# Another order of turns for five instruction streams in a 32-unit fused kernel

## The reference

```python
x = x + L0_attn(layernorm(x))   # 16 heads; q and k become spike counts (0 to 4) in 4 steps
x = x + L0_ffn(layernorm(x))    # gated, inputs, weights and hidden values rounded to FP4 in blocks of 16
x = x + L1_attn(layernorm(x))   # four Mamba layers, below
x = x + L1_ffn(layernorm(x))    # ternary weights, hidden size 512, silu and gelu
x = x + L2_attn(layernorm(x))   # causal linear attention, 16 heads
x = x + L2_ffn(layernorm(x))    # 8 experts, hidden size 512, top 1
x = x + L3_attn(layernorm(x))   # long convolution as a scan, gelu, projection, norm
x = x + L3_ffn(layernorm(x))    # dense part plus product-key experts
```

```python
u  = silu(conv(x @ Wi.T));  dt, B, C = split(u @ Wx.T);  dt = softplus(dt @ Wdt.T + bdt)
h  = exp(dt * A) * h + dt * B * u        # step by step over 256 tokens, 256 channels x 16 states
y  = (h * C).sum(states) + u * Dp;       out = (y * silu(z)) @ Wo.T + x
```

## Time and profile before

| what | us |
|---|---|
| median of 3 runs | 1852.78 |
| lowest, highest run | 1848.98, 1853.91 |
| span of the profiled execution | 1849.7 |
| PE busy | 1481.9 (80%) |
| DVE busy | 1499.8 (81%) |
| ACT busy | 1345.1 (73%) |
| POOL busy | 1196.0 (65%) |
| mean granted clock of TensorE | 0.879 of 2.4 GHz |

### The profile page before, as it was taken

The page is one execution under the profiler, slowest core; times in us unless marked ns, Lnnn a source line. Parts: engine busy times, 40 slices in busy tenths (PEclk is TensorE's granted clock), DMA queues, the critical chain, the costliest instruction groups (busy, mean ns, idle before and its releaser), DMA issues.

```text
span 1849.7 us, 27473 instructions
## 1 busy us (share of the span) xinstructions
PE 1481.9 (80%) x9417; PEld 1054.5 (57%) x9417; DVE 1499.8 (81%) x2326; ACT 1345.1 (73%) x2733; POOL 1196.0 (65%) x999
## 2 busy tenths in 40 slices
PE   5767666667898998577778999778899987889975
PEld 2433333335676666454456787656667765667854
DVE  6589999999999899978898888888889999731254
ACT  4466756666988788767687978788888787654564
POOL 3247668667676688866665656788878778730046
PEclk6667877778999999777798999999999998889997
DMA  5022403423444434220244444341445432212300
GB/s 194 1 69 70 121 18 95 113 70 103 115 117 119 126 104 110 72 69 24 64 119 123 117 127 134 92 112 49 127 136 141 132 104 70 66 33 85 115 18 6
DMA packets 84585, 170.10 MB, mean 92 GB/s; under 512 B 9440, under 2 KB 14944, under 8 KB 84064
## 3 DMA queue, kind: packets, MB, share of 16 engines
q1 hardware_dynamic: 84448, 168.37, 33.4%
HBM read 99.12 MB, written 2.10 MB: 55 GB/s over the span
## 4 chain that ended last, share of the span: by engine, by line
PE 42%; DVE 22%; ACT 19%; POOL 7%; issue 6%; DMA 3%; SPq 1%; DVEq 0%; POOLq 0%; ACTq 0%
DVE m L1051 8%; ACT m L1026 6%; DVE dtuB L1043 5%; PE ps L1080 4%; PE ps L1182 4%; PE ps L1467 3%; PE ps L1476 3%; PE ps L1314 3%; PE ps L965 3%; DMA m<-m 3%; PE ps L1764 3%; ACT L347 2%; PE ps L698 2%; PE ps L1325 1%; PE ps L711 1%
## 5 line engine op out<-in xcount | busy, mean ns | idle before, releaser
L1061 POOL TENSOR_TENSOR m<-m 128x1024 f32<-128x1024 f32 x256 | 777.2, 3040 | 162.8 <-DVE m L1051 161.1
L1051 DVE TENSOR_TENSOR_SCAN m<-m,dtuB 128x1024 f32<-128x1024 f32 x256 | 584.5, 2283 | 22.7 <-ACT m L1026 9.3
L1026 ACT ACTIVATE m<-m,Aneg 128x255 f32<-128x255 f32 x1024 | 431.7, 499 | 26.0 <-DMA m<-m 18.2
L1043 DVE TENSOR_TENSOR dtuB<-m 128x1024 f32<-128x1024 f32 x256 | 348.9, 1363 | 9.7 <-DMA m<-m 3.2
L1467 PE MATMUL ps<-o 128*128 128x256 f32 x512 | 150.8, 406 | 17.9 <-DVE X L1411 7.1
L1080 PE MATMUL ps<-m,w_const 128*32 128x256 f32 x2048 | 154.6, 432 | 12.1 <-POOL m L1061 12.1
L1434 ACT ACTIVATE o<-ps,w_mo 128x256 f32<-128x256 f32 x256 | 114.8, 472 | 54.9 <-PE ps L1467 54.0
L364 POOL TENSOR_TENSOR o<-o,mhalf 128x2 f32<-128x2 f32 x64 | 19.6, 306 | 200.0 <-DVE o L358 199.9
L965 PE MATMUL ps<-m,wc 128*128 128x256 f32 x512 | 134.3, 421 | 7.4 <-ACT m L385 7.3
L1476 PE MATMUL ps<-o 128*128 128x128 f32 x1024 | 130.6, 281 | 4.9 <-ACT o L1434 4.1
L1476 PEld LDWEIGHTS ps<-o 128*128 128x128 f32 x1024 | 124.5, 195 | 14.8 <-ACT o L1434 9.5
(11 more groups left out here) (251 smaller groups left out, 2920.1 us busy)
## 6 DMA issues: line engine op xcount, KB each, us to landing
m<-m SPq DMA_DIRECT2D x256, 256.0 KB, 4.8
m<-spread SPq DMA_DIRECT2D x64, 512.0 KB, 4.8
o<-in_mox SPq DMA_DIRECT2D x128, 256.0 KB, 2.9
o<-in_l1x SPq DMA_DIRECT2D x88, 256.0 KB, 2.9
w_mb<-in_mb SPq DMA_DIRECT2D x1, 2288.0 KB, 11.7
m<-in_cwr SPq DMA_DIRECT2D x1, 2048.0 KB, 15.8
w_l3f<-in_l3f SPq DMA_DIRECT2D x1, 1536.0 KB, 17.5
X<-in_x SPq DMA_DIRECT2D x4, 256.0 KB, 6.4
```

What stands on the lines that cost most here:

```text
L1026: op = e.activation(dA[at % NA][:, j, 1:CH], R[q][:, h * CH + 1:h * CH + CH], ACT.Exp, scale=Aneg[:, l, 4 * g + j:4 * g + j + 1])
L1043: e.tensor_tensor(dtuB[:, :, :], bc(R[q][:, (2 + h) * CH:(3 + h) * CH].unsqueeze(1), 4, CH), Br[k % 2], ALU.mult).then_inc(S.dve, n.tick(f ...
L1051: e.tensor_tensor_scan(flat(G[at % NG]), flat(dA[at % NA]), flat(dtuB[:, :, :]), 0.0, ALU.mult, ALU.add).then_inc(S.dve, n.tick(f"s{g}"))
L1061: e.tensor_tensor(G[at % NG], G[at % NG], Cr[k % 2], ALU.mult).then_inc(S.pool, n.tick(f"c{g}"))
```

## The change

Only the five strings of `ORDER` differ. The number of turns of each line on each engine is the same, and so are instructions, waits, tiles and DMAs, except table loads: ACT has 188 of them in its stream before (with one for each change of set) and 187 now. The first lines of two of the strings:

```diff
     "pe":
-        "a9ua2ua3ba2ba7bab2ab8ab2ab2ab5a3bab2a2f2b3faf2bab2abasa4b2a3fa2f2af2sa2bab2abab2asb2fab4sfabfsaf2bfsb2fsab2af2af3"
+        "a15uaubaba6b2abab8ab2a2b7a3bab2a2f2b2abf3ab3aba8fbaba2f3sfa2sab4a2b2sab2fab3asb2fafbsf3sb3fsa2f4bafb2sa2ba2babas"
...
     "dve":
-        "aua7u2bu3b7a11ba2fb2fb3a7b5fb2fs3fsbs2bs2bs4b2sb2fs8fs2af2s8a2sfa2fasf2s4as5a2sa2fs2abas2bs3a2bafasabababs2f2s6b"
+        "a2ua4uauab6ub2aua5ua5ba2fb2fb3a7b5fb2fs3fs9b7sfs8fs2fafs9a2fa2fasf2s8as2a4fs2a2bs2b2s3b3a3f3a4s9bs2b4fs7fs3f2sas8"
```

More of the change, by code:

```diff
@@ L214 @@
+        "s3fs4b5f3sbs5b2s2b2s4f2sfs6f2sfs4afsf2s7a5f3a2s8a4f3bs2b2s6b4f3s6b3sbsa3bafafa2sfs7a6fb2a2fabs8b2fb10f2s3bsfs4f2"
+        "a4s5a3fa3s2a2sf2sfs6b4sf3b2s2b2s3bsbs2a3b2a2faf2s4as2as2f3a2s8a3bafb2f2asbsbs4basb2sb2fb2fsbsfsbsbsbs3fs5fs2fsa12"
+        "b12a12ba2b2abab13a",
     "pe":
-        "a9ua2ua3ba2ba7bab2ab8ab2ab2ab5a3bab2a2f2b3faf2bab2abasa4b2a3fa2f2af2sa2bab2abab2asb2fab4sfabfsaf2bfsb2fsab2af2af3"
-        "b2sa3bab2a2safbabasa5fafbfa2fsfa6sa2fasaf2b2sfafafb2sb2fa2fsfbf2bfb2sb8sb2afsb4fsf3bfbsfsa2bf3asf2b2asfa2sbababa2"
@@ new lines @@
+        "afasb3fabafa3fabfba2fa2sab2a2ba2b2a2ba3b3a2sb2abababa2fababa2fba2fbabafafabfbs2ba2b2a5b5sbabfb4ab2fb2fb2fab3afabf"
+        "b2a2b2abasb3sab2ab8sa2fba3f2bf2afasa2bababa2sb2a2b2a2sa2fa3b2a2f2b4afasfa2bsfa4b2a3bab2asabafba2bfafbabfafafs2b2"
+        "a2b2sbabafba2babasafafsfafafbabasa2fb2a2b3fa2fbfasfb2a2fsbab3ab4sabfa2babf2ab2sa2fafa2b2fb2sb3aba2b3ab2sab2fb6afb"
+        "fbsb2fa2fsfab6ab5sb2afb4fsa3bafafafafsba4baba2b3sabafbsa5b2a5b4aba3sa3b3ababsa3fa3bab2a2ba3ba3b2abababab2ababa5b"
+        "a2b3aba2b2a2ba2b3a2b3ab3a3b2a2baba4baba3bab5aba2b2a3b6ab3a2bab4ab11ab8a2ba3ba2b3ab2ab2a5b7a2baba2b3",
@@ new lines @@
+    "dve":
+        "a2ua4uauab6ub2aua5ua5ba2fb2fb3a7b5fb2fs3fs9b7sfs8fs2fafs9a2fa2fasf2s8as2a4fs2a2bs2b2s3b3a3f3a4s9bs2b4fs7fs3f2sas8"
+        "a2fb2faf2a2sb7s10afs10fs2f2s9ba3f2af2s3fs13bafbafb3sf2safasbasab3sbs6fb2s7a2bfsf2s2a3b2sbas5fs10fs2f2as3babas3ab2"
+        "s2afsbabsfs2f2as8as4fsabsfs2af2b2s2abs4as3asabs2fba2s2bas2a2fbf2s8bs5bfa6fa2sf2as2bs3as2ba2s3b2sa6b2a2sfbas2b2sas"
+        "a2s3a2fs2f2sba6bfab2s2b4s2b2sb2fs4b8abs3fba2f2b2a2fab2sas4b7s8fa4fs2f2asas6as2as2bas2ab2fsb3fs3f2s2bs7b4a2fs2b2s4"
+        "a3fabf2b2s5bs4fs7af2asafs2babs2as4asb3fbsas4as5fas3f2asbs2ab3s2fabs2a2s2bfsaf2abasa2bs5bs4faba7bas3abs2ababfsf2ab"
+        "fsa5ba2sbasb2asasas3fa2s2a2s2as2ab6sb2f3bs3bfba2sbs4b4a2sab4abfs4b3sb2s3f3s2bs2bs2abs2a2s2fbs4as2fs2f2as8b2as3fba"
+        "bf3b2s5as8fs4as2fbf2s2babs2bs4bs2fas2bs4bfsaf2bs5bs6afabsba2s2fsabf2sa2bsbs6a3b2a6bsbabfasas3a5saba2fb2as2abfa2b2"
+        "s2a2b2s2baba2b2as4bs2b8sasab3sa3fbafb5a4b2abab3a2bab2ab2abab2a2babababa2b4aba2b2a6b3a2b3ab3a5b3a4b7ab2a2b3ab",
@@ new lines @@
+    "act":
+        "a11bua3u3baba5bab3ab5ab2a2b5aba2bafabf2ab2fbf2afbab2asasafa2sasfab2sfabas2f2af2a2bsb2sabsbsa2b2sbs2b2fafbs2f4ab2"
+        "s2afsbfs2af3asb2sfbsa3ba3sbs2bsa4fa2fasasbf2bf2asbsa3s2asa2s2a2f2s3fab2f3ab3fsfs2ba2f3sbsfbs3b4sbsb2s2b2sb4fbs2fs"
+        "af4s2afs2af2s2af2s2fbfba2sbsafa2bfabfs3a2fb2fa2bfsfs2a2sbababs2a3fafaba2bfabfsfas2fas2ababsasab2asas2asb2f2b2asfa"
+        "bafb3fsafa3bab3sba2sba2s2bafbabfs2ba2f2sbfsfa4b2asa2bas2a4fbfbsa4s2fba2fa2fsfb4a2b2s2b2asb2ab2sabasafb2abfs3fab2f"
+        "sfb2fbabasb2safbasb3fs2af2bab3asa2babf2bs2a2bas2ab2a2s2b2a2sab2faf2ba2safbabfsafasfab3a2ba2ba3ba2s2b2ab2abfbafbfb"
+        "as2fbafsfsfbsbsb8sb2asa2bsb2fsfsasabafabfs2fa2bfaba2sab2s3afafs2f2ba2fsfb3a2sa2b2s3a2ba2b2f2bafafsfas2afbabsasasa"
+        "bab2sas2babfbfasfabafab2fa2sfba2b2a2bsab2a2sabsab2sasba2bs2ba4bsfba2fsa2fbfabfba2fabsa4b3sbs2bababsbab2fb2fasbfa"
+        "b2fbasafab2fb2a3b4s2a2b4sb4a3babsfas2f2asbf2abfafa3sbabs2ba4b2a2bs2ba2sa3b2afa2bfbfbs2bafabfa2bfa2s2fa3b2sabababa"
+        "bs2basabsbaf2bs2afbfabfsfsab2asb2s2ab2sa2sb2sa2f2s2f2bafa2bfab2sa2b3asbfbfas3f2ba2fsbasafb2sb2sb2sasa3bf2s2babfa2"
+        "fasfbsfb2ab2saba2bsb3sb2sbsb3f2bs2fab2abfsfa2fbsb3abasb4as2b2ab2sf2a2sab2as2fafa2fsfba2ba2ba2b2a2bs3ba2b2a4s2a2b2"
+        "a2b2a2ba2bsba3bsa3b2sb2ababa7bab2a2b2a2ba2bab2ab3a2b2a2ba3b5ab2a3b2a2b3a2b3a2ba2ba4b2a4b5a4b7a2b2abab2ab3ab5ab4a"
+        "b4a3b2ababa2b3ababab2a3babab5a2b2a2babab3",
@@ L254 @@
+        "fbs5afas2a2sfs7fa4fa3sasasas2bsa2ba2fba4ba2s3asaf2sb4ab4s2b2fs3b9abf2b2s3bs5f2sas6bfs2fs4afsbs2asfs3fs5afsbs3bfs3"
+        "fs4bs2fs2afa2sas5fa7sa2sabfbsfsa4ba6bsfas5b3sbfb5fbsas3b4ab2sb3fbs2bsfs4asfs3fs4bs3f2bs6fs3fsbs4fs3fs6fasa2sfasb"
+        "s3ba5ba4bafs3a10b3sab6sbs4b9abs2ba2b3a4b4a10b10a8b4ab2ab4",
 }
```

43 lines of the change are left out of this document (6 added, 37 removed).

## The result

The changed kernel is slower: 1869.24 us at the median of its four runs (1866.63 to 1873.23) against 1853.1 us for the kernel before, run beside it (1848.98 to 1853.91). The ratio is 1.0096 with a 95% interval of 1.0077 to 1.0115: 14 to 21 us more, where I had forecast 8 us less. 1869.24 lies outside my range as well. The profiled execution took 1866.63 us, its span is 1864.8.

A forecast was written before the change was run, and what follows sets the result against it. DVE, busy 89% of the scan stage, was taken to set the pace; its terms of -10.7 us times 0.89 gave -9.5, with +0.5 and +1.0 -8.0: 1844.8 us from 1852.78, eight-in-ten range 1824 to 1861.

The forecast's parts named there:

- (a): First scan unit on DVE: turns of line b leave the gaps between groups, two held L1043 go; -4.3 us.
- (b): Other scan places with turns between L1051 and L1043: fewer holds of L1043 by new counts; -3.3 us, ends 0 and -10.1.
- (c): L838's waits on DVE at 898.95 and 1381.81 us are filled by other turns; -3.1 us, bounds -3.1 and +3.1.
- (d): Head on DVE: 25 setup instructions lose their covering wait and run ahead of L748; +0.5 us, ends 0 and +2.5.
- (e): POOL in the scans: L1061 takes 1.03 us longer at 14 more places; +1.0 us, ends 0 and +14.4.
- POOL takes over: Rival 2: in stretches of eight groups POOL has no time left, so the front comes late; +6.8 us, 1859.6, chance 0.09.
- the sum of +6.8 us: Scans, holds only moved between DVE and POOL: -7.6 us on DVE plus 14.4 us on POOL.
- (f): Table loads, one fewer of 188, nothing; tail, PE's work is the same and turns swap: 0, ends -3 and +3 us.
- The factor 0.89: DVE's busy share in the scan stage, taken as the part of its -10.7 us that counts: -9.5 us.
- the fifth: Whole order: turns are put ahead of others that are ready sooner, without the gains; +6.6 us, 1859.4, chance 0.05.
- rival 3: PE's granted clock falls to 0.69 in a scan stretch; +11 us, 1855 with the gain or 1864 without, chance 0.05.

The follow-up runs named there:

- e8_b_turns: Kernel before with one DVE move: seven turns of sequence 3's L0Attn stand together behind the first scan unit's sixth group; 0.9970, -5.6 us.
- e14_l838: Kernel before with seven DVE turns at 898.95 us in the new order, L409 and L411 ahead of L838 among them; 1.0014, +2.6 us.
- e10_act_1350: Kernel before with 23 ACT turns from 1348 us reordered, the first norm of unit 27's front five turns later; 1.0027, +5.0 us.
- e3_late: Kernel before with the new order of all engines from 1301 to 1630 us only (units 25 to 31); 1.0022, +4.1 us.
- e11_1682: Kernel before with the new order of all engines from 1682 to 1725 us only, in the tail; 1.0023, +4.3 us.
- e9_middle: Kernel before with the new order of all engines from 616 to 1301 us only (units 12 to 24); 1.0041, +7.6 us.

## Why the prediction was wrong

The mechanism I knew best was right, and it was a small part of the change. By my own steps:

- (a), -4.3: right in kind, sign and size. Both holds are gone; e8_b_turns gives -5.6 us, and unit 1's first L1043 starts at 148.27 there; I had said 147 to 148. In the changed kernel it starts at 153.84, 2.2 us later than before, because the first scan starts 7.7 us late: that hid the gain.
- (b), -3.3: wrong. L1043's excess over 1.232 us fell from 33.5 to 256 x (1.346 - 1.232) = 29.2 us, and these 4.3 us are no more than (a) alone. I had carried one mean per kind of place over to new places. In the changed kernel the places with one turn between have 0.48 instead of 0.60, those with two 0.20 instead of 0.10, and the 196 with none 0.10 instead of 0.09, 18 of them over 1.5 us instead of 13. Whether L1043 is held depends on where POOL is, not on the count of turns: of those over 1.5 us, 29 of 30 before and 28 of 28 now started while a POOL instruction had over 0.3 us still to run, and at the others that was so at 10 of 226 and 18 of 228.
- (c), -3.1 with bounds of ±3.1: the value wrong, and the bound far too tight. The wait at 898.95 fell from 3.82 to 2.00 us as I had said, and brought nothing (e14_l838). The place at 1381.81 became one of the worst: the front of unit 27 comes late on ACT, 5.0 us, and the wait that I had counted as filled went to L841 (L839 now), which the prediction had named as its own sign of being wrong. The sentence "some turns now stand ahead of turns that were ready sooner, which the trace of before can't price; bounds of (c) are -3.1 and +3.1" took a size from the gains that I had found. The middle and the late units measure +7.6 and +4.1.
- (d), +0.5 with an end at +2.5: the step that failed most. It looked at the 25 instructions of L536 to L546 alone. The turns of Setup on DVE also hold the weight rounding, some 11.5 us of work, and its cover, the first wait for ACT, was gone: DVE's order of the head is worth +7.0 us. My own test was "wrong if L748 starts later than 58.5 us". It starts at 68.2, 10.4 us late. The 25 instructions themselves did what (d) said: they run from 63.3 to 68.2, in 4.9 us, the rounding ahead of them ends 10.4 us late as well, and so they add nothing.
- (e), +1.0 with an end at +14.4: harmless. L1061's busy time went from 777.2 to 776.0 us, its mean from 3.04 to 3.036 instead of the forecast 3.10; POOL's wait for L1051 fell by a quarter, to 122.3. With it falls the rival "POOL takes over". The price of 1.03 us a place was also too high by my own rows: where L1043 was held, L1061 took 2.72, not 2.35, which leaves 0.66. The holds went on as before, with POOL's L1059 of 136.80 at 2.44 us and the spike counts issued behind it at 4.50. The rule of the Trainium skill (SBUF — State Buffer, section "Who interferes with whom") that the two operations shut each other out and the issue order decides fits this, but the sum of +6.8 us by way of POOL isn't what happened.
- (f), 0 with ends of ±3 for the tail: wrong, +10.8 us. I reasoned from PE's stage sum, which indeed hardly moved (120.8 and 119.24 us), and not from the line that ends last.
- The factor 0.89 for how much of DVE's saving counts: DVE lost 23 us of busy time in the scan stage and gained 23 us of idle time. Over the stage the share was zero. This step lies under all the DVE terms: I took the busiest engine for the one that ends the stretch. Where DVE did end it, in the first scan unit, the saving arrived in full (e8_b_turns); elsewhere it became idle time.

The right rival was the fifth, a search on a wrong picture, which had 0.05. Its price of +6.6 was put together from the plus ends of (c), (d) and (e), and so inherited bounds that were too tight: 20.7 us lost and won by stretches, +17.8 in all. The clock, rival 3, isn't the cause: 0.89 in the scan stage in both, 0.97 and 0.96 behind it, 0.87 and 0.85 at the end. In the first 110 us it rose from 0.67 to 0.83, more than the 0.1 that I had named as a sign of being wrong, and the first scan came later all the same.

What stays open: which places make the +7.6 us of the middle, and the 6.5 us of the tail outside 1682 to 1725 us. PE's tail order by itself wasn't tried, nor the weight rounding apart from DVE's other turns of the head. The smaller losses (e3_late, e10_act_1350, e11_1682) have intervals that begin within 1 us of zero.

## What to carry to other kernels

Price a reordering by the turns that each chain's next step waits for, from the first row to the last, not by the fullest engine's holds: a long instruction group that leaves its cover, a short one that the next front needs and that is put behind a table load, and a product of the line that ends first put ahead of the line that ends last cost 7.0, 5.0 and 4.3 us here, as much as the clearest gain promised (4.3) or more. For the first and the last the cost is that of the stretch they stand in. Where a table of turns is split at places with equal counts, the stretches can be timed one by one, and the good one kept: here the new order of units 0 to 11 alone is 9.8 us faster than before. An edit whose loss can't be priced from the trace needs a bound from what such chains carry, not from the gains beside it.

## What the runs showed of the hardware

One kernel's executions spread more than I had thought: e3_late took 1849.09 to 1877.75 us in twelve runs. Its profiled one, of 1875.81 us, shows why. From 1655 to 1685 us, first in it, then in the kernel before:

```profile
1655.00:1685.00 30.00, 30.00 (x122) 21.49 (x121) 1.94 (x4) 8.31 (x13) 0.00 (x0) 0.50 0.05 18
```
```profile
1655.00:1685.00 30.00, 29.17 (x178) 23.51 (x177) 6.06 (x27) 12.28 (x26) 2.36 (x8) 1.00 0.31 97
```

PE was busy nearly without a gap in both, as it had been from 1640 to 1655 (13.1 and 13.6 of 15 us), but its granted clock was 0.50, the 1.2 GHz level, in the one, with 122 products, and 1.00, 2.4 GHz, in the other with 178. At that place it cost 13 us (22.4 less 9.2: the lag of line b behind the kernel before grows from 9.2 us at the end of the last scan to 22.4 us at the end of L1Ffn of sequence 7), more than any stretch of the order did. What made the clock fall there in this execution no run shows. Smaller shifts are in every trace: with the same old order ahead of it the first scan starts at 102.8 us in one of them (e9_middle) and between 106.2 and 108.7 in the others. A change of 4 us therefore needs the medians of a dozen runs, and a single pair of traces tells where, but not how much.
